# GpSimd raises a variance to the power -1/2 in place of Newton steps on DVE, in a fused MoE / attention / MoE kernel

## The reference, cut to what matters

```
x = x + 0.5 * ffn(layernorm(x))      # router picks one of 8 experts per row, relu^2 MLP 128 -> 512 -> 128
x = x +       attention(layernorm(x))# 16 heads of 8 channels, windows 128, 64, ..., 4; v = k; gated; projected
x = x + 0.5 * ffn(layernorm(x))

layernorm(x) = (x - mean(x)) / sqrt(var(x) + 1e-5)     # over the 128 channels of a row
```

## Time and profile before

| what | us |
|---|---|
| device time, median of 3 runs | 521.06 (518.32 to 521.98) |
| span of the profiled execution, first to last instruction | 509.5 |
| PE busy | 416.1 (82%) |
| DVE busy | 351.6 (69%) |
| ACT busy | 285.9 (56%) |
| POOL busy | 228.6 (45%) |

### The profile page before, as it was taken

The page is one execution under the profiler, slowest core; times in us unless marked ns, Lnnn a source line. Parts: engine busy times, 40 slices in busy tenths (PEclk is TensorE's granted clock), DMA queues, the critical chain, the costliest instruction groups (busy, mean ns, idle before and its releaser), DMA issues.

```text
span 509.5 us, 10040 instructions
## 1 busy us (share of the span) xinstructions
PE 416.1 (82%) x2836; PEld 387.8 (76%) x2837; DVE 351.6 (69%) x728; ACT 285.9 (56%) x875; POOL 228.6 (45%) x197
## 2 busy tenths in 40 slices
PE   2941999999967888966999789895696869999990
PEld 2941999999946877856787788785685869989990
DVE  5866445458755899797979699999984385545550
ACT  2340677677647455735566568683352645766760
POOL 4057750350257763642407033425176155777551
PEclk9999999999999676969779699897565797999996
DMA  8971332242128450604306041403022712462210
GB/s 263 398 212 51 104 113 67 82 114 71 52 59 177 97 122 1 148 20 83 83 17 152 0 94 54 85 17 68 15 101 93 188 40 84 122 172 61 55 46 0
DMA packets 85357, 48.17 MB, mean 95 GB/s; under 512 B 45874, under 2 KB 80314, under 8 KB 85073
## 3 DMA queue, kind: packets, MB, share of 16 engines
q1 hardware_dynamic: 80272, 37.32, 28.5%
q0 software_dynamic: 5056, 10.52, 6.6%
HBM read 25.66 MB, written 22.98 MB: 95 GB/s over the span
## 4 chain that ended last, share of the span: by engine, by line
PE 49%; DVE 27%; POOL 9%; issue 7%; DMA 4%; ACT 2%; POOLq 0%; DVEq 0%; SPq 0%; ACTq 0%
PE bank L1246 16%; PE bank L1237 16%; DVE osh L996 4%; POOL late_rows_d L473 4%; PE bank L1356 3%; PE bank L1324 3%; DVE nmax L956 3%; POOL rows_d L473 2%; PE bank L1228 2%; PE bank L1305 2%; DVE newton L818 2%; DVE rstd L819 2%; DVE rows L791 2%; PE bank L1212 1%; DMA xs<-late_rows_d 1%
## 5 line engine op out<-in xcount | busy, mean ns | idle before, releaser
L1246 PE MATMUL bank<-wo,hT 128*128 x736 | 102.6, 284 | 5.9 <-ACT hT L600 5.8
L894 DVE TENSOR_SCALAR hT<-bank 128x512 f32<-128x512 f32 x92 | 63.6, 692 | 59.9 <-PE bank L1237 59.4
L1237 PE MATMUL bank<-xT,fcb 128*128 128x128 f32 x736 | 101.8, 284 | 0.7 <-ACT xT L584 0.7
L1246 PEld LDWEIGHTS bank<-wo,hT 128*128 128x128 f32 x736 | 91.4, 196 | 7.2 <-issue 6.6
L1237 PEld LDWEIGHTS bank<-xT,fcb 128*128 128x128 f32 x736 | 93.8, 200 | 1.5 <-ACT xT L584 1.5
L594 ACT ACTIVATE fcb<-fc 128x512 f32 x92 | 57.7, 630 | 52.6 <-PE bank L1237 52.6
L678 ACT ACTIVATE late<-bank,nmax 128x128 f32<-128x128 f32 (+1 forms) x128 | 50.1, 395 | 26.7 <-DVE nmax L956 21.6
L600 ACT ACTIVATE hT<-hT 128x512 f32<-128x512 f32 x92 | 57.6, 626 | 10.7 <-DVE hT L894 10.5
L483 POOL DMA_INDIRECT out_rows<-late x46 | 45.2, 983 | 38.7 <-DVE late L903 30.1
L1324 PE MATMUL bank<-kT,qT 128*128 128x128 f32 (+4 forms) x256 | 56.0, 354 | 0.0
L1324 PEld LDWEIGHTS bank<-kT,qT 128*128 128x128 f32 x256 | 49.1, 226 | 3.8 <-issue 0.5
(11 more groups left out here) (130 smaller groups left out, 841.2 us busy)
## 6 DMA issues: line engine op xcount, KB each, us to landing
ks<-k_d SPq DMA_DIRECT2D x32, 192.0 KB, 3.3
late_rows_d<-hT SPq DMA_DIRECT2D x5, 1028.0 KB, 7.5
rows_d<-late SPq DMA_DIRECT2D x2, 1472.0 KB
xs<-rows_d SPq DMA_DIRECT2D x23, 128.0 KB
y_d<-ys SPq DMA_DIRECT2D x46, 64.0 KB
xs<-late_rows_d SPq DMA_DIRECT2D x23, 128.0 KB
late<-late_rows_d SPq DMA_DIRECT2D x2, 1225.5 KB, 6.9
fc<-in_w_fc SPq DMA_DIRECT2D x1, 2048.0 KB, 16.9
```

Of the source, the lines that this page charges most:

```text
L894: nc.vector.tensor_scalar(hT[:, v, :, :].rearrange("p k c -> p (k c)"), bank[v][:, :], 0.0, None, ALU.max).then_inc(r_s, 1)
L1237: mm = pe.matmul(bank[v][:, k * 128:(k + 1) * 128], fcb[:, v, k * 128:(k + 1) * 128], xT[:, v, :], start=True, stop=True)
L1246: mm = pe.matmul(bank[OUT_BANK[f] + v][:, 0:128], hT[:, v, k, :], wo[:, ds(e, 1), k, :], start=(k == 0), stop=(k == KT - 1))
```

## The change

Six calls of `spread` in the attention stretch become `scaled_variance`, which keeps only the first of the 11 DVE instructions (L810, without a wait behind it). GpSimd gets one new instruction per group, `roots`: a tensor_tensor with the operation pow, of the group's 8, 12 or 4 columns of `var` and a constant tile of -0.5. In windows 1 and 3 `roots` stands ahead of `normalise_batch`, and in windows 3 to 6 ahead of `normalise`. The constant is filled by one more memset among the first instructions of GpSimd. The other groups keep Newton steps, and waits on counts of the semaphores are moved to match.

```diff
+        minus_half = sb("minus_half", [128, MOST])
...
-            eng.wait_ge(rstd_s, len(SEG[0]) + 1 + [4 * i < tiles.stop for tiles in LN2].index(True))
+            late = [4 * i < tiles.stop for tiles in LN2].index(True)
+            if late:
+                eng.wait_ge(root_s, late)
+            else:
+                eng.wait_ge(rstd_s, len(SEG[0]) + 1)
...
+            pool.memset(minus_half[:, :], -0.5).then_inc(cleared_s, 1)
...
+            def roots(k, tiles):
+
+                pool.wait_ge(eps_s, k)
+                pool.tensor_tensor(rstd[:, tiles], var[:, tiles], minus_half[:, 0:len_of(tiles)], ALU.pow).then_inc(root_s, 1)
+
             def window(i):
                 if i > 0:
                     light_products(pool, i, i % 2)
+                if i in (1, 3):
+                    roots(i // 2 + 1, LN2[i // 2 + 1])
                 if i + 2 < B:
                     normalise_batch(pool, i + 2)
                 if i == 1:
                     centre(LN2[2])
                     squares(6, LN2[2])
                 if 3 <= i < 7:
-                    normalise(pool, 1, len(SEG[0]) + len(LN2) + 1 + i - 3, batch(i - 3))
+                    roots(i, batch(i - 3))
+                    normalise(pool, 1, (root_s, i), batch(i - 3))
...
+            def scaled_variance(n, tiles):
+
+                dve.wait_ge(var_s, n + 1)
+                nc.vector.tensor_scalar(var[:, tiles], var[:, tiles], 1.0 / C, EPS, ALU.mult, ALU.add).then_inc(eps_s, 1)
...
-                (0, 5): lambda: variance(5, LN2[1]), (0, 6): lambda: spread(5, LN2[1]),
+                (0, 5): lambda: variance(5, LN2[1]), (0, 6): lambda: scaled_variance(5, LN2[1]),
...
-                (2, 1): lambda: variance(6, LN2[2]), (2, 4): lambda: spread(6, LN2[2]),
+                (2, 1): lambda: variance(6, LN2[2]), (2, 4): lambda: scaled_variance(6, LN2[2]),
...
                     if n == (6 if i == 2 else 5) and i < 6:
-                        spread(7 + i - 2, batch(i - 2))
+                        scaled_variance(7 + i - 2, batch(i - 2))
...
-            dve.wait_ge(cleared_s, 6)
+            dve.wait_ge(cleared_s, 7)
```

More of the change, by code:

```diff
@@ L212, in macaron @@
         rstd_s = sem("spread_known")
+        eps_s = sem("variance_ready")
+        root_s = sem("inverse_root_ready")
         norm_s = sem("rows_normalised")
@@ L343, in normalise @@
         def normalise(eng, f, r, tiles):
-            eng.wait_ge(rstd_s, r)
+            eng.wait_ge(*r)
             eng.wait_ge(rt_px_s, GROUPS * f + tiles.stop // RG)
@@ L546, in _ @@
             put_out(range(0, EARLY_OUT))
-            normalise(pool, 1, len(SEG[0]) + len(LN2) + 6, SEG[1][1])
+            normalise(pool, 1, (rstd_s, len(SEG[0]) + 3), SEG[1][1])
             scatter(1, 1, SEG[1][1], 8)
@@ L1104, in _ @@
             centre(LN1[3])
-            normalise(nc.vector, 0, 1, SEG[0][0])
+            normalise(nc.vector, 0, (rstd_s, 1), SEG[0][0])
             count_blocks(0, 0, 4)
@@ L1112, in _ @@
             choose(0, 1, 3)
-            normalise(nc.vector, 0, 2, SEG[0][1])
+            normalise(nc.vector, 0, (rstd_s, 2), SEG[0][1])
             count_blocks(0, 1, 3)
@@ L1157, in _ @@
             spread(11, batch(4))
-            normalise(nc.vector, 1, len(SEG[0]) + len(LN2) + 5, batch(4))
+            normalise(nc.vector, 1, (rstd_s, len(SEG[0]) + 2), batch(4))
             gate(B - 1)
@@ L1413, in _ @@
             pe.wait_ge(const_s, 16)
-            pe.wait_ge(cleared_s, 6)
+            pe.wait_ge(cleared_s, 7)
             pe.wait_ge(route_w_s, 16)
```

## The result

The changed kernel took 498.86 us (median of 4 runs, 496.32 to 499.92) and the kernel before 520.78 (median of 4, 518.32 to 521.98) beside it. The ratio is 0.963, 95% interval 0.958 to 0.968: faster by 19.5 us, between 17 and 22. The prediction said 9.1 us, a time of 512.0 and a lower end of 500. The sign was right, the size less than half.

What follows compares the result with a forecast made beforehand. DVE's Newton groups, stalled by POOL, were taken to bound the attention stretch. Removal -15.4, gate stalls +6.1 and memset +0.2 gave -9.1 us, so 521.06 became 512.0 us, range 500 to 521.

Steps and rivals of the forecast that it cites:

- What bounds the kernel: Attention stretch: DVE sets the pace in six Newton groups, 29 us of the chain, each running into POOL once.
- Removed, with what is late next: Newton steps gone from DVE: its fold moves forward until POOL's product ends, gaining 15.4 of the 29 us.
- Added on POOL: Six pows on POOL at 1.0 us each, between 0.13 and 5.17; POOL's own time costs nothing.
- Moved, onto the path, +6.1 us: After POOL's product, xb, pow and normalise take turns with DVE's gate, giving back 6.1 us.
- What lies around the span, 11.6 us,: Time between the profiled span of 509.5 us and the median of 521.06, left as it is.
- The clock: TensorE's slow phases, 4.3 us each, stay unchanged in number; two more or fewer (8.6 us) as bounds.
- Rival 2: Time comes back through PE: windows 5 and 6 fall into slow phases, 520.6 us; chance 0.20.
- Rival 1: Nothing holds DVE up, the fold slips in ahead of POOL's product: full gain, 492 us; chance 0.10.
- Rivals 3 and 4: Pow long and DVE stands still: 536 us, chance 0.10; first pow alone long, 5.17 us: 514.4, chance 0.10.

Runs made afterwards that it cites:

- after_third: The changed kernel, unchanged, run again in a session where the kernel before takes 592 us: ratio 0.977 to the kernel before.

## Why the prediction was wrong, step by step

**What bounds the kernel** held: DVE was on the path in the Newton groups, each ran into POOL once, and 29 us of the chain were theirs. By the Trainium skill, "SBUF — State Buffer", section "Who interferes with whom", a DVE instruction with two SBUF inputs contends with a GpSimd instruction that reads SBUF; the ports that they share are an exclusive lock, and issue order decides who blocks. By that rule the trace agrees for product, part, normalise and bias add (5.09 us under 5.20); for pow, which reads SBUF as well, it differs, and the measurement decides. Why a pow lets DVE through isn't shown.

**Removed, with what is late next** was right in kind and too small by 4.3 us: 19.7 against 15.4. The fold does go forward until it meets the product's end (window 2: forecast 7.7, measured 7.7; window 3: 4.2 and 4.5). Window 0 gave 4.7 instead of 2.5 in the pair, of which its gate stretch took back 1.2, and nothing against the repeats of the kernel before; window 4 gave 2.4 instead of 1.0, since the product started 9.0 us after the bias add there (286.64 - 277.7) and not 10.4, as in the kernel before (305.23 - 294.9).

**Added on POOL**: 1.0 us was right for 4 columns; 8 and 12 took 1.67 and 2.29 and lay beside other work. POOL did not idle 11 us before every L334, as the text has it: in window 1 it was 3.39 us before the change and 2.08 after, still not negative. The ratio that the prediction took from the Trainium skill, "GPSIMD Engine Reference", section 4.1, gave 0.34 us; the trace shows three to seven times that for pow.

**Moved, onto the path, +6.1 us, is the step that failed** as a mechanism. It let xb, pow and normalise each take turns with DVE's gate, "and 5 us more per further microsecond of pow". The runs show 0 for a pow, even of 8 us. What is left is the normalise: 0.7 us in windows 3 and 4 and 0.8 in window 5, 2.2 in all. With 2.2 for 6.1 the sum would have been -13.0. So this step and the size of the one on what is removed weigh about the same, 3.9 and 4.3 us.

**What lies around the span, 11.6 us,** was misread too. In all later runs 1.8 to 2.4 us lie there; the rest was that one short execution. It didn't move the forecast of -9.1 us, since it was added back unchanged. Whether a sum made on an ordinary execution would have come out larger isn't shown: the fold stretches of the repeats, 98.1 and 94.1, are about the 97.1 of that one. With the measured fold stretches (19.7), the normalise (2.2) and 0.2 for the memset the sum is 17.3 us, the lower edge of the measured 17 to 22. What the other 2 us are stays open.

**The clock** was left unchanged, and the gate sums of several executions show no more than a small loss to it. Rival 2 is seen in the profiled pair alone (windows 4 and 5, +2.4 and +4.7 us), and not in the medians. Rival 1 had the right direction and too much of it. Rivals 3 and 4 fell: no pow was long (the first, of 8 columns, took 1.67 us and lies on the line of the others), and none held DVE. Nor was there a gap around the first pow: POOL's product ended at 184.85, the pow ran from 184.81 to 186.48, and xb began at 186.56.

## What to carry to other kernels

When a chain of tiny instructions on DVE costs far more than their sum, look for the long GpSimd instruction that they run into: either take their work off DVE or let GpSimd start when the chain is done, for one wait in the right place was worth about as much here as the change itself (16 to 21 us on top of it). Before costing a new instruction as a partner in such a collision, ask whether it is one; a pow is not. And check the profiled execution's own time against the median: where it lies 10 us below, look which stretches ran at a better clock than they usually do.

## What was not expected of the hardware

- GpSimd's pow takes 0.36 us and 0.16 us a column of 128 partitions (1.00, 1.67, 2.29 and 8.04 us for 4, 8, 12 and 48), and DVE's instructions with two SBUF inputs run beside it at full speed, while they stand still behind GpSimd's multiply and add. So do DVE's scalings with one input: L811 for 3.36 us behind the product, L844 for 1.20 behind the part.
- DVE and GpSimd alternate instruction by instruction: beside four pieces of 384 columns, four steps of DVE took 0.78 us each.
- The same kernel took 519 us in some sessions and 592 to 596 in others, on either chip. Most of the added time is idle and lies in the feed-forward stages, and the profile puts part of it down to a releaser outside of what it shows: in after_third ScalarE's L610 alone (fcb) waited 41.8 us so in 6 waits, the longest 12.8, and the changed kernel's first trace has no such wait among ScalarE's seven longest. Why is open.

Whether Newton temporaries in PSUM would escape the collision wasn't tried.
